# A group's query and key stacks by six transfers of 4 KB pieces, and the distance attention's head loop written out

## What is computed

```
kh = (k @ Wk.T + bk) split into 16 heads; qh likewise, with the same Wk
scores = qh @ kh.T / sqrt(DH)
p   = softmax(where(mask, scores, -1e32)) * mask
cum = cumsum(p);  tot = sum(p)
dist = sqrt(clip((tot - cum) * |i - j|, 0))
total_effect = clip(exp(dist * -softplus(gamma) * exp(sigmoid(pdiff))), 1e-5, 1e5)
out = softmax(where(mask, scores * total_effect, -1e32)) @ vh     # row 0 is set to 0
```

## Time and profile before

| | |
|---|---|
| median of 3 runs | 3367.78 us (3362.89 to 3376.7) |
| profiled execution | 3377.88 us, its span 3376.0 us |
| granted clock of PE, mean | 0.917 of full speed |
| L0x attention | about 97 to 386 us |
| L2x attention | about 1670 to 1905 us |
| L3x attention | about 2480 to 3270 us |
| DMA: packets, MB, mean | 161801, 326.75 MB, 97 GB/s |

### The profile page before, as it was taken

The page is one execution under the profiler, slowest core; times in us unless marked ns, Lnnn a source line. Parts: engine busy times, 40 slices in busy tenths (PEclk is TensorE's granted clock), DMA queues, the critical chain, the costliest instruction groups (busy, mean ns, idle before and its releaser), DMA issues. The chain is left out here.

```text
span 3376.0 us, 47872 instructions
## 1 busy us (share of the span) xinstructions
PE 2814.2 (83%) x14850; PEld 1587.6 (47%) x14944; DVE 1901.4 (56%) x4752; ACT 1728.7 (51%) x2884; POOL 850.3 (25%) x957
## 2 busy tenths in 40 slices
PE   6799849779999997656699888999768788888877
PEld 3233339734444444323222358998424444444443
DVE  5777621255555555105588631112588988898963
ACT  3566411146555553001277532332468988898863
POOL 4100020110000000002200030002457777777750
PEclk9899959989999999778799999999869989898998
DMA  4111236520000000892121138996410000000101
GB/s 164 44 53 46 59 140 217 177 71 1 1 1 1 1 1 25 343 416 89 56 63 60 62 140 302 344 346 219 152 48 20 20 16 19 25 15 14 26 24 51
DMA packets 161801, 326.75 MB, mean 97 GB/s; under 512 B 29408, under 2 KB 128480, under 8 KB 138208
## 3 DMA queue, kind: packets, MB, share of 16 engines
q1 hardware_dynamic: 150544, 301.64, 25.4%
q0 software_dynamic: 4608, 12.59, 1.1%
q10 hardware_dynamic: 6480, 10.49, 0.9%
HBM read 275.22 MB, written 49.28 MB: 96 GB/s over the span
## 5 line engine op out<-in xcount | busy, mean ns | idle before, releaser
L2911 DVE TENSOR_TENSOR_SCAN L3x_behind<-L3x_first_exp,L3x_beside_scan 128x513 f32<-128x513 f32 x256 | 309.6, 1209 | 20.8 <-issue 20.8
L2792 POOL TENSOR_TENSOR L3x_fade<-L3x_behind,L3x_apart 128x1024 f32<-128x1024 f32 x128 | 280.0, 2187 | 161.6 <-DVE L3x_mx L2929 106.4
L1265 ACT ACTIVATE L1x_probs<-L1x_scores,L1x_neg_max 128x512 f32<-128x512 f32 x256 | 173.5, 683 | 226.6 <-DVE L1x_neg_max L1319 226.6
L1319 DVE TENSOR_REDUCE L1x_neg_max<-L1x_scores 128x2 f32<-128x1024 f32 x128 | 156.6, 1224 | 142.9 <-PE L1x_scores L1154 142.9
L2717 PE MATMUL L3x_probs_tp<-identity,L3x_fade 128*128 128x128 f32 x1024 | 170.4, 292 | 61.6 <-POOL L3x_neg_max_parts L2801 59.4
L1607 ACT ACTIVATE L2f_hiddenT<-L2f_hidden_ps,L2f_b1s 128x128 f32<-128x128 f32 x320 | 99.9, 363 | 209.0 <-PE L2f_hidden_ps L1542 209.0
L2829 ACT ACTIVATE L3x_first_exp<-L3x_scores,L3x_nm 128x512 f32<-128x512 f32 x256 | 180.4, 705 | 38.8 <-DVE L3x_nm L2903 36.2
L783 DVE CUSTOM_DVE_ANT_0 L0x_masked_scores<-L0x_s,L0x_mask_q 128x512 f32<-128x512 f32 x256 | 167.1, 685 | 56.7 <-issue 56.5
L2717 PEld LDWEIGHTS L3x_probs_tp<-identity,L3x_fade 128*128 128x128 f32 x1024 | 133.3, 151 | 139.6 <-POOL L3x_neg_max_parts L2801 91.3
L2857 ACT ACTIVATE L3x_probs_T<-L3x_probs_tp 128x512 f32<-128x512 f32 x256 | 157.9, 617 | 62.8 <-PE L3x_probs_tp L2720 62.8
L2903 DVE TENSOR_REDUCE L3x_nm<-L3x_scores 128x1 f32<-128x512 f32 x256 | 173.2, 677 | 29.1 <-remote 22.4
(11 more groups left out here) (530 smaller groups left out, 6257.7 us busy)
## 6 DMA issues: line engine op xcount, KB each, us to landing
L2f_w1s<-in_L_w SPq DMA_DIRECT2D x40, 1024.0 KB, 7.6
L2f_w2s<-in_L_w SPq DMA_DIRECT2D x40, 1024.0 KB, 6.5
L1f_w1s<-in_L_w SPq DMA_DIRECT2D x32, 1024.0 KB, 15.6
L1f_w2s<-in_L_w SPq DMA_DIRECT2D x32, 1024.0 KB, 10.7
L0f_w1s<-in_L_w SPq DMA_DIRECT2D x16, 1024.0 KB, 6.3
L0f_w2s<-in_L_w SPq DMA_DIRECT2D x16, 1024.0 KB, 5.2
L0x_q_stack<-L0x_q_parts SPq DMA_DIRECT2D x96, 64.0 KB, 2.7
L0x_k_stack<-L0x_k_parts SPq DMA_DIRECT2D x96, 64.0 KB, 2.7
```

The costliest lines, as they stand in the source:

```text
L1265: nc.scalar.activation(p[:, n % 3, h, :], s[:, n % 2, h, :], ACT.Exp, bias=nmax[:, n % 4, h:h + 1], accum_out=den[:, n % 4, h:h + 1]).then ...
L2792: nc.gpsimd.tensor_tensor(fz[:, f:f + 2, :], bs[:, fb:fb + 2, 0:S], w, ALU.mult).then_inc(y_done, 1)
L2911: nc.vector.tensor_tensor_scan(bs[:, f, :], ex[:, t, :], beside[:, 0:1].to_broadcast([P, S + 1]), 0.0, ALU.add, ALU.bypass).then_inc(f_don ...
```

## The change

1. `q_parts` and `k_parts` are laid out by part, batch, block of 128 rows, row, token, and the 128 rows of a block are now ordered by element and then by head (16 x 8 in place of 8 x 16). For that the columns of wq, wk (wk alone in L3), their biases, the rotation matrix and the tables of angles are reordered on the host (`heads_inside`, `both_ways`); their shapes stay. The four heads of a group thus stand side by side in DRAM for each of the 16 elements, 4 KB.
2. `Stacks.load` takes three runs instead of six row blocks: leading query part three times against the key's three parts (48 rows), middle query part twice against two key parts (32 rows), last query part against the leading key part (16 rows). A query run is a broadcast of one part. That makes 6 transfers a group; `LOADS` is halved. Between the projections' stores one run is loaded after each.
3. In `distance_attention`, `run` has no loop any more.

```
-    def load(self, sp, b, hg, rows=range(6)):
+    def load(self, sp, b, hg, runs=range(3)):
         dk, half = 16, hg % 2
-        for r in rows:
-            for st, part, src in ((self.q, (0, 0, 1, 1, 0, 2)[r], self.qs), (self.k, (0, 1, 0, 1, 2, 0)[r], self.ks)):
-                sp.dma_start(st[r * dk:(r + 1) * dk, 4 * half:4 * half + 4, :],
-                             src[part, 4 * hg * dk:4 * (hg + 1) * dk, ds(b * S, S)].rearrange("(h r) t -> r h t", r=dk)
+        for n in runs:
+            first, rows = (0, 3, 5)[n], 3 - n
+            for st, src in ((self.q, self.qs[n:n + 1]), (self.k, self.ks[0:rows])):
+                at = src[:, b, hg // 2, :, :].rearrange("p (r h) t -> p r h t", r=dk)[:, :, 4 * half:4 * half + 4, :]
+                to = st[first * dk:(first + rows) * dk, 4 * half:4 * half + 4, :]
+                sp.dma_start(to.rearrange("p h t -> p (h t)"),
+                             at.rearrange("p r h t -> p r (h t)").to_broadcast([rows, dk, 4 * S])
                              ).then_inc(self.loaded[half], 16)
...
-                    to = dest[d][:, m * P:(m + 1) * P, b * S:(b + 1) * S].rearrange("n p t -> p n t")
+                    to = dest[d][:, b, m, :, :].rearrange("n p t -> p n t")
...
-                        stacks.load(sp, 0, n // 3, range(n % 3 * 2, n % 3 * 2 + 2))
+                        stacks.load(sp, 0, n // 3, range(n % 3, n % 3 + 1))
...
-    LOADS = 16 * 12
+    LOADS = 16 * 6
...
-    qs = c.scratch(tag + "q_parts", (3, HD, N), BF16)
-    ks = c.scratch(tag + "k_parts", (3, HD, N), BF16)
+    qs = c.scratch(tag + "q_parts", (3, B, HD // P, P, S), BF16)
+    ks = c.scratch(tag + "k_parts", (3, B, HD // P, P, S), BF16)
...
         def run(eng, body):
 
-            for k in range(-2, 8):
-                body(k, k % 8, k // 2)
-            with eng.Fori(1, 7) as r:
-                for i in range(8):
-                    body(r * 8 + i, i, r * 4 + i // 2)
-            for k in range(56, U + 6):
+            for k in range(-2, U + 6):
                 body(k, k % 8, k // 2)
...
+    def heads_inside(v):
+
+        n = v.shape[-1]
+        return a(np.swapaxes(v.reshape(-1, n // P, 8, 16), 2, 3).reshape(v.shape))
+
     def both_ways(table):
 
-        t = np.tile(np.repeat(table, 2, axis=1).T, (8, 1))
+        t = np.repeat(np.repeat(table, 2, axis=1).T, 8, axis=0)
```

More of the change, by code:

```diff
@@ L2621, in distance_attention @@
     qst, kst, group_loaded = stacks.q, stacks.k, stacks.loaded
-    LOADS = 12 * 16
+    LOADS = 6 * 16
     mq, am, vsum = mask
@@ L3108, in host_layout @@
         "mask0": mask0, "mask0T": a(mask0.T),
-        "L0_bq": cols(i["L0_xattn_bq"]), "L0_bk": cols(i["L0_xattn_bk"]), "L0_bv": i["L0_xattn_bv"],
+        "L0_bq": cols(heads_inside(i["L0_xattn_bq"])), "L0_bk": cols(heads_inside(i["L0_xattn_bk"])), "L0_bv": i["L0_xattn_bv"],
         "L0_bo": i["L0_xattn_bo"],
@@ L3112, in host_layout @@
         "L1_bo": i["L1_xattn_b_o"], "L1_ln_g": i["L1_xattn_ln_g"], "L1_ln_b": i["L1_xattn_ln_b"],
-        "L2_wqT": a(i["L2_xattn_Wq"].T), "L2_wkT": a(kv[:, 0].reshape(D, D).T), "L2_wvT": a(kv[:, 1].reshape(D, D).T),
+        "L2_wqT": heads_inside(a(i["L2_xattn_Wq"].T)), "L2_wkT": heads_inside(a(kv[:, 0].reshape(D, D).T)),
+        "L2_wvT": a(kv[:, 1].reshape(D, D).T),
         "L2_woT": a(i["L2_xattn_Wo"].T),
-        "rope_rotT": a(rot.T), "rope_cos": both_ways(np.cos(ang)), "rope_sin": both_ways(np.sin(ang)),
+        "rope_rotT": heads_inside(a(heads_inside(rot).T)), "rope_cos": both_ways(np.cos(ang)), "rope_sin": both_ways(np.sin(ang)),
     }
@@ L3136, in host_layout @@
     for n in ("Wk", "Wv", "Wo"):
-        d["L3_" + n.lower() + "T"] = a(i[f"L3_xattn_{n}"].T)
-    d["L3_bk"], d["L3_bv"] = cols(i["L3_xattn_bk"]), i["L3_xattn_bv"]
+        w = a(i[f"L3_xattn_{n}"].T)
+        d["L3_" + n.lower() + "T"] = heads_inside(w) if n == "Wk" else w
+    d["L3_bk"], d["L3_bv"] = cols(heads_inside(i["L3_xattn_bk"])), i["L3_xattn_bv"]
     d["L3_bo"] = i["L3_xattn_bo"]
@@ L3150, in host_layout @@
     for n in ("wq", "wk", "wv", "wo"):
-        d[f"L0_{n}T"] = a(i[f"L0_xattn_{n}"].T)
+        w = a(i[f"L0_xattn_{n}"].T)
+        d[f"L0_{n}T"] = heads_inside(w) if n in ("wq", "wk") else w
         d[f"L1_{n}"] = i[f"L1_xattn_w_{n[1]}"]
```

## The result

| | before | after |
|---|---|---|
| median of 4 runs | 3370.27 us (3362.89 to 3376.7) | 3597.16 us (3590.88 to 3600.08) |
| ratio, 95% interval | | 1.0664 [1.0636, 1.0692] |
| span of the profiled execution | 3376.0 us | 3597.8 us |
| granted clock of PE, mean | 0.917 | 0.893 |

The changed kernel is slower by 227 us. The forecast was 3528 us, with a range of 3440 to 3610: sign and range held, and the sum was 67 us short.

The account below looks back on a forecast made before the run. PE was taken to bound L0x and L2x, and DVE, with ACT close behind, L3x. Terms 68 + 59 + 15 + 18 = +160 us on the profiled 3377.9 gave 3538, forecast as 3528 us; range 3440 to 3610.

Parts of the forecast that it names:

- I take 3, 2 and 16 engines: Stack loads: each transfer runs on as many DMA engines as its DRAM side's first dimension; 42 completion packets a group, not 192.
- The landing: Stack loads: a group lands 13.4 us after its first issue in L3x, 13.1 us in L0x and L2x.
- L3x, loads: longer waits: Distance attention: PE waits 7.6 us for stacks instead of 2.5, costing DVE 5.1 us in each of 14 groups: 72 us.
- L3x, loads: lower clock: Distance attention: longer idling puts PE on the lower clock in 7 more groups, 2.4 us each: 17 us.
- L3x, loop written out: Distance attention: straight code removes 5 loop edges, idle times of DVE: -21 us, bounds 0 to -21.
- first two groups of each stage: Loads between the last projections delay the stores of the parts: 6 us in each of three stages, 18 us (0 to 30).
- I take 4.2, the wait and half the clock's cost: L2x, a plain attention: PE waits 3.0 us a group plus part of the lower clock; 14 x 4.2 = 59 us (31 to 76).
- a wait of 1.1 us: 14 x 1.1 = 15: L0x, a plain attention: PE waits 1.1 us for stacks in each of 14 groups: 15 us (0 to 49).
- Rival 1: Stack loads use all 16 engines and the change is faster: 3307 us; chance 0.10.
- Rival 2: Few engines, but only L3x pays; L2x's wait and the first groups are hidden: +68 us, 3436 us; chance 0.12.
- Rival 3: Distance attention: written-out code stalls where the loop did, so the 21 us don't come: 3549 us; chance 0.15.
- The point at which the sign turns: Landing time of a group at which longer waits cancel the 21 us from the loop: 9.8 us after first issue.

Follow-up runs that it names:

- experiment 1: The changed kernel's six transfers with the 16 elements ahead of the copies on the DRAM side: 3304.95 us, ratio 0.9792 to the kernel before.
- experiment 4: The changed kernel with the 16 elements first on the DRAM side for the 48-row loads only, 32-row loads left on two engines: 3408.34 us.
- experiment 3: The changed kernel with twelve transfers a group again, each of 16 rows of one 4 KB piece: 3345.88 us, ratio 0.9911 to the kernel before.
- experiment 5: The changed kernel with the distance attention's loop put back: 3631.34 us, ratio 1.0784 to the kernel before.
- experiment 2: The kernel before with the distance attention's loop written out and nothing else: 3350.69 us, ratio 0.9928.

## Why the forecast was right, and where it was short

**Engines per transfer: right.** The step on which the sign rested was "I take 3, 2 and 16 engines". The completions are 42 a group. In the stretch of L3x there are 636 small packets after, 1392 in experiment 1, 1000 in experiment 4 and 2736 in experiment 3: 48 for three stores, and 14 times 42, 96, 68 and 192. From the list of DMA packets, L3x after:

```profile
DMA packets 4922, 13.32 MB, mean 16 GB/s; under 512 B 636, under 2 KB 2172, under 8 KB 4860
```

And in experiment 1:

```profile
DMA packets 5678, 13.33 MB, mean 18 GB/s; under 512 B 1392, under 2 KB 2928, under 8 KB 5616
```

The open point, 48 rows in the stack against 3 parts in DRAM, is thereby settled: in these patterns the smaller first dimension decides. The rule of the Trainium skill, page "DMA: Bandwidth & Descriptors", section "Why a DMA increments its semaphore by 16 and not by 1", by which both sides count, agrees with all four counts. The advice in the same page's "Rules for kernel authors", to coalesce small transfers, is worth 41 us here (experiment 3 against 1), once the pattern is spread over 16 engines.

**The landing: short by 1 us, and that is paid 42 times.** I sized it at 13.1 and 13.4 us; it is 14.2. My 10.5 us for the bytes of the busiest engine was 11.5 in the group shown, with 1.3 us ahead of the first byte and 1.0 behind the last. I took the rate from a stretch in which all 16 engines ran; here 270 KB in 11.5 us are 23.5 GB/s for the busiest one, not 25.8.

| term | forecast | measured |
|---|---|---|
| L3x, loads: longer waits | 72 | 87 (121.8 - 34.7) |
| L3x, loads: lower clock | 17 | 17 (what is left of 104; not measured apart) |
| L3x, loop written out | -21 | -35 (experiment 5) |
| L3x together | 68 | 70 |
| L2x | 59 | 83 |
| L0x | 15 | 48 |
| first two groups of each stage | 18 | 23 |
| sum | 160 | 224 |

**L3x: the right number by two errors.** The loop form with the new loads takes 888.2 us and the loop form before 783.8: the loads cost 104 us, not 89. The wait is what I had too small: PE's waits for the stacks are 89 us longer there (123.6 against 34.7), where I had 72, because a group lands 14.2 us after its first issue and not 13.4, and PE is ready 5.5 us after that issue in the changed kernel and not 5.8. The clock's 17 us (15 by these waits) are only a remainder. The written-out form gives back 35, not 21, since it shortens DVE's clips too. That a late group costs DVE its whole delay is confirmed by rows like these of after, around one such wait (DVE, start, us, instruction, idle time before it):

```profile
3141.24 0.69 DVE L2901 TENSOR_REDUCE L3x_nm<-L3x_scores 128x1 f32<-128x512 f32 x1 [6.32 <-PE L3x_scores L2695]
...
3145.45 0.06 DVE L2926 MEMSET L3x_gate<- 128x1 f32 x1 [2.39 <-PE L3x_scores_again L2695]
...
3147.91 0.69 DVE L2901 TENSOR_REDUCE L3x_nm<-L3x_scores 128x1 f32<-128x512 f32 x1 [1.72 <-PE L3x_scores L2695]
```

The last two are the pair of the earlier trace rows, which came with the lower clock; they now come every time (PE's first matmul takes 0.61 us in all 14 groups), and the 6.32 us are new.

**L2x and L0x: the term that failed.** The steps "I take 4.2, the wait and half the clock's cost" and "a wait of 1.1 us: 14 x 1.1 = 15" were mis-sized. PE was ready when I said, 10.1 and 12.0 us after the first issue. But the wait was 3.9 and 2.3 us, by the longer landing; and I had counted the clock at 1.2 us a group in L2x and at nothing in L0x, where it costs 30 / 14 = 2.1 and at most 18 / 14 = 1.3. Together 5.9 and 3.4 us a group. In L0x the granted clock fell from 0.98 to 0.93 with waits of 1.5 to 4.1 us. L0x came out at the end of its bounds (0 to 49), L2x beyond them (31 to 76): I had let the clock add 2.4 us at most to a wait of 3.0, and the wait alone was 3.9.

**Loop edges:** the five idle times of 4.1 us are gone, as forecast. What I didn't see is that the heads of the loop had slower clips: the row was there before (DVE's L2936, 1295 ns on the mean, 1123 in experiment 2), and I had compared only idle times, not the durations of the same instruction in and out of the loop. Experiment 2 hides it, because a faster DVE ran into the late loads (waits 8.9 us longer).

**Rivals.** Rival 1, all 16 engines, forecast 3307; experiment 1, which makes it true, gives 3305. Part of that is luck: the L3x waits were still 20.6 us, and writing out the loop brought more than the 21 us of its edges. Rival 2 fell: L2x and L0x together lost 131 us. Rival 3 fell: no gap at DVE every few heads. The point at which the sign turns, 9.8 us of landing, fits the runs: 8.1 us is faster by 0.9%, 10.6 us slower by 1.0%.

## What to carry to other kernels

Before merging transfers, look at the first dimension of the pattern on *both* sides, and count the completion packets of one transfer in the trace: a broadcast or a part index of 3 in front moved 192 KB through 3 engines, and swapping two letters in the pattern was worth 292 us. When a load gets late, take the distance between landing and need in each stage, and price PE's clock in every one of them where PE now waits, not only in the one where you first saw it. And when comparing a loop with its written-out form, compare the duration of the same instruction as well as the idle times, since the loop shifts what runs beside it on another engine.

## What the runs showed of the hardware

- Two or three engines with 4 KB pieces move 49 to 74 GB/s, where 16 reach 412 GB/s; the busiest one needed about 11.5 us for 270 KB, 23.5 GB/s.
- Issuing a transfer of 48 or 32 rows takes SP's queue 0.61 to 0.71 us in the group of the changed kernel, and 0.55 to 0.59 us in that of experiment 1, against 0.30 to 0.43 us for one of the twelve. (Of the two 16-row transfers among the six, the query's takes 0.55 to 0.58 us and the key's 0.41.) Six issues therefore take 3.5 us in experiment 1, not half the time of twelve (5.5 us).
- The same matmuls kept PE busy 30 us longer in L2x (226 to 256 us), after 14 waits of 3.2 to 4.9 us; the granted clock of the stage fell from 0.96 to 0.86.
- DVE's clip of 128 x 1024 takes 0.68 us alone, and ends 0.55 us after POOL's product when that runs: 1.15 to 1.85 us mostly, and 2.52 us at most.
